# Reordering the opening of a ternary feed-forward kernel: q and W2 in two parts, the weights' sums and transposes placed inside the third and fourth product

## What is computed

```
q   = relu(cond @ W3 + b3)                       # 128 x 256
c   = relu(((32*x + sum_s x) * q[:, None, :]) @ W2 + b2)
wKq = ternary(wK), K = 1, 2, 3: s = mean|w|; clip(round(w / s), -1, 1) * s
out = x + (silu(c @ w1q.T) * (c @ w3q.T)) @ w2q.T
```

## Time and profile before

| | us |
|---|---|
| median of 3 runs | 165.79 (165.62 to 165.82) |
| the profiled execution's own time | 165.22 |
| its span, first to last instruction | 163.4 |
| PE busy | 159.5 (98% of the span) |
| DVE busy | 118.7 (73%) |
| ACT busy | 89.1 (55%) |
| POOL busy | 55.1 (34%) |

### The profile page before, as it was taken

How to read it: one execution, slowest core, us unless ns; L and a number is a source line. 1 busy time by engine, 2 the same in 40 slices (tenths; PEclk the granted TensorE clock), 3 DMA queues, 4 the chain that set the end, 5 groups by cost and what they waited for, 6 DMA issues and landing times.

```text
span 163.4 us, 2290 instructions
## 1 busy us (share of the span) xinstructions
PE 159.5 (98%) x760; PEld 131.0 (80%) x760; DVE 118.7 (73%) x190; ACT 89.1 (55%) x163; POOL 55.1 (34%) x53
## 2 busy tenths in 40 slices
PE   8999999999999999999999999999999999999992
PEld 4798777888887888788887888788887888788892
DVE  1698999988978892798458891788548870566863
ACT  4077889344845375445844475345844466255540
POOL 5014022502460276205750276204841266001500
DMA  5998656665666599200240007000150006000163
GB/s 138 330 337 161 95 83 98 97 98 85 97 98 98 89 201 169 34 4 0 49 79 0 4 0 128 2 0 0 35 96 4 2 0 117 12 0 0 21 112 128
DMA packets 67412, 12.67 MB, mean 78 GB/s; under 512 B 63216, under 2 KB 67144, under 8 KB 67400
## 3 DMA queue, kind: packets, MB, share of 16 engines
q1 hardware_dynamic: 67248, 12.46, 39.2%
q10 hardware_dynamic: 152, 0.07, 0.2%
HBM read 8.32 MB, written 4.19 MB: 77 GB/s over the span
## 4 chain that ended last, share of the span: by engine, by line
PE 97%; DVE 1%; issue 0%; DVEq 0%
PE bank L553 50%; PE bank L596 22%; PE bank L483 15%; PE bank L580 3%; PE bank L469 2%; PE bank L518 1%; PE bank L445 1%; PE bank L498 1%; PE bank L452 1%; PE bank L510 0%; DVE qT L769 0%; PE bank L492 0%; PE bank L443 0%; DVE x L682 0%; DVE xo L821 0%; PE bank L521 0%
## 5 line engine op out<-in xcount | busy, mean ns | idle before, releaser
L553 PE MATMUL bank<-c_hi,T 128*128 128x512 f32 (+1 forms) x176 | 69.2, 393 | 0.0
L553 PE MATMUL bank<-c_lo,T 128*128 128x512 f32 (+1 forms) x176 | 68.8, 391 | 0.0
L389 ACT ACTIVATE silu<-bank,checked 128x512 f32<-128x512 f32 (+1 forms) x48 | 33.1, 689 | 51.5 <-PE bank L553 51.4
L806 DVE SCALAR_TENSOR_TENSOR gf<-bank,out_scale,silu 128x512 f32<-128x512 f32 (+1 forms) x42 | 31.2, 744 | 34.4 <-PE bank L553 30.8
L553 PEld LDWEIGHTS bank<-c_hi,T 128*128 128x128 f32 (+1 forms) x176 | 32.8, 186 | 7.6 <-issue 0.2
L553 PEld LDWEIGHTS bank<-c_lo,T 128*128 128x128 f32 (+1 forms) x176 | 32.8, 186 | 7.3
L272 POOL TENSOR_TENSOR x<-y,qT 128x512 f32<-128x512 f32 x12 | 13.7, 1144 | 53.2 <-DVE y L711 53.2
L596 PE MATMUL bank<-g_hi,T 128*128 128x512 f32 x70 | 28.5, 407 | 0.0
L814 DVE TENSOR_TENSOR g_lo<-gf,g_hi 128x512 fp32r<-128x512 f32 x40 | 28.5, 711 | 0.0
L396 ACT CAST g_hi<-gf 128x512 fp32r<-128x512 f32 x40 | 24.5, 612 | 5.4 <-DVE gf L806 5.1
L596 PE MATMUL bank<-g_lo,T 128*128 128x512 f32 x70 | 27.3, 390 | 0.0
(11 more groups left out here) (81 smaller groups left out, 118.1 us busy)
## 6 DMA issues: line engine op xcount, KB each, us to landing
xb<-in_x_dram SPq DMA_DIRECT2D x64, 64.0 KB, 2.5
out_dram<-turned SPq DMA_DIRECT2D x28, 128.0 KB, 2.7
xo<-in_x_dram SPq DMA_DIRECT2D x3, 256.0 KB, 4.4
w_sb<-in_L_ffn_w_dram SPq DMA_DIRECT2D x2, 384.0 KB, 5.5
w_sb<-in_L_ffn_w_dram SPq DMA_DIRECT2D x1, 682.0 KB, 7.8
w_sb<-in_L_ffn_w_dram SPq DMA_DIRECT2D x2, 256.0 KB
xo<-in_x_dram SPq DMA_DIRECT2D x1, 512.0 KB, 4.7
xo<-in_x_dram SPq DMA_DIRECT2D x2, 128.0 KB, 2.4
```

The costliest lines, as they stand in the source:

```text
L389: nc.scalar.activation(silu[r, m % 2, :], h1[j % 2][r], ACT.Silu, scale=checked[r, 0:1]).then_inc(silu_done, 1)
L553: last = pe.matmul(dst[j % 2][0:w, :], T13[:, k, col:col + w], part[:, g % NC, k, :], start=(i == 0), stop=(i == len(passes) - 1))
L806: nc.vector.scalar_tensor_tensor(out=gf[r, m % 3, :], in0=second, scalar=out_scale[r], in1=silu[r, m % 2, :], op0=ALU.mult, op1=ALU.mult). ...
```

## The change

- SP issues W2 as two loads with a semaphore each, and x half 3 between w1's first and second piece.
- `project_q` takes the sequences it works on. The first call, at its old place, makes q of halves 0 and 1 (16 sequences); the second, of the other 112, takes the place of `keep_busy(3)`. DVE adds bias and relu for the 16, ACT for the 112. `scale_mixed` waits for the latter.
- PE does `sum_partitions(0)` between the two chunks of `project_c(2)`, and w1's first transposes with `sum_partitions(1)` between the two chunks of `project_c(3)`.
- w3's first transposes move behind `h1_step(0)`, then `h1_step(1)`, then `h3_step(0)`, w1's other blocks, `h3_step(1)`, w3's other blocks and `sum_partitions(2)`.
- On DVE `scale_mixed(3)` moves ahead of `limit(0)` and `above_limit(0)`.

```diff
-            def load_w13(w_sb, w, got):
+            def load_w13(w_sb, w, got, between=None):
                 cut = LOADED * P
                 sp.dma_start(w_sb[:, 0:LOADED, :], ...).then_inc(got[0], 16)
+                if between is not None:
+                    load_half(between)
...
-            sp.dma_start(W2_sb[:], ...).then_inc(got_W2, 16)
+            for k in range(DC):
+                sp.dma_start(W2_sb[:, k], W2[k * P:(k + 1) * P, :]).then_inc(got_W2[k], 16)
             load_half(2)
-            load_w13(w1_sb, w1, got_w1)
-            load_half(3)
+            load_w13(w1_sb, w1, got_w1, between=3)
...   (ScalarE, ahead of relu(0))
+            act.wait_ge(q_done, 2 * DC)
+            for c in range(DC):
+                nc.scalar.activation(qT[:, HALVES:NH, c, :], q_rest_ps[:, c]..., ACT.Relu,
+                                     bias=b3_col[c]).then_inc(q_rest_ready, 1)
...   (TensorE, project_c)
                 for c in range(DC):
+                    if c and n == 2:
+                        pe.wait_ge(const_ready, 4)
+                        pe.wait_ge(q_rest_ready, DC)
+                        sum_partitions(0)
+                    if c and n == 3:
+                        pe.wait_ge(x1_done, EARLY - 1)
+                        transpose_w13(0, 0, w1_t)
+                        pe.wait_ge(q_ready, DC)
+                        sum_partitions(1)
...
             mix_x(0)
-            keep_busy(3)
+            project_q(q_rest_ps, slice(QF, B))
             mix_x(1)
-            pe.wait_ge(got_W2, 16)
             project_by_parts(0)
             mix_x(2)
             project_by_parts(1)
             mix_x(3)
-            sum_partitions(0)
             project_c(2)
-            transpose_w13(0, 0, w1_t)
-            sum_partitions(1)
             project_c(3)
-            transpose_w13(1, 0, w3_t)
...
             h1_step(0)
+            transpose_w13(1, 0, w3_t)
+            h1_step(1)
             h3_step(0)
             transpose_w13(0, 1, w1_t)
-            h1_step(1)
+            h3_step(1)
             transpose_w13(1, 1, w3_t)
             sum_partitions(2)
-            h3_step(1)
...   (VectorE)
             early_lo(0)
+            scale_mixed(3)
             limit(0)
             above_limit(0, w1_sb, w1_t, parts[0])
-            scale_mixed(3)
             limit(1)
```

More of the change, by code:

```diff
@@ L53, in adaln_ternary_ffn_kernel @@
     QB = P // BT
+    QF = HALVES * HB
     HTB = HT // BT
@@ L132, in adaln_ternary_ffn_kernel @@
         b_cols_ps = bank[:, 3, 0:2 * DC]
-        qT_ps = bank[:, 5, 0:DC * B].rearrange("p (c b) -> p c b", c=DC)
+        q_first_ps = bank[:, 5, 0:DC * QF].rearrange("p (c b) -> p c b", c=DC)
+        q_rest_ps = bank[:, 4, 0:DC * (B - QF)].rearrange("p (c b) -> p c b", c=DC)
         sums_ps = [bank[:, b, 0:2] for b in (4, 5, 7)]
@@ L146, in z_of @@
             return bank[:, b, :].rearrange("p (c n) -> p c n", c=DC)
-        got_cond, got_W3, got_W2, got_b = sem("got_cond"), sem("got_W3"), sem("got_W2"), sem("got_b")
+        got_cond, got_W3, got_b = sem("got_cond"), sem("got_W3"), sem("got_b")
+        got_W2 = [sem(f"got_W2_{k}") for k in range(DC)]
         got_w1, got_w3 = [[sem(f"got_w{k}_{part}") for part in range(2)] for k in (1, 3)]
@@ L163, in adaln_ternary_ffn_kernel @@
         b_cols_done, b_cols_copied = sem("b_cols_done"), sem("b_cols_copied")
-        q_done, q_ready = sem("q_done"), sem("q_ready")
+        q_done, q_ready, q_rest_ready = sem("q_done"), sem("q_ready"), sem("q_rest_ready")
         abs_done, sums_done, limit_done = sem("abs_done"), sem("sums_done"), sem("limit_done")
@@ L223, in _ @@
             load_half(1)
-            sp.dma_start(W2_sb[:], W2.rearrange("(c p) n -> p c n", p=P)).then_inc(got_W2, 16)
+            for k in range(DC):
+                sp.dma_start(W2_sb[:, k], W2[k * P:(k + 1) * P, :]).then_inc(got_W2[k], 16)
             load_half(2)
             sp.wait_ge(zeroed, 2)
-            load_w13(w1_sb, w1, got_w1)
-            load_half(3)
+            load_w13(w1_sb, w1, got_w1, between=3)
             load_w13(w3_sb, w3, got_w3)
@@ L322, in _ @@
             act.wait_ge(b_cols_copied, 1)
+            act.wait_ge(q_done, 2 * DC)
+            for c in range(DC):
+                nc.scalar.activation(qT[:, HALVES:NH, c, :], q_rest_ps[:, c].rearrange("p (h b) -> p h b", b=HB), ACT.Relu,
+                                     bias=b3_col[c]).then_inc(q_rest_ready, 1)
             def relu(n):
@@ L435, in mix_x @@
                         transpose_b()
-                        project_q()
+                        project_q(q_first_ps, slice(0, QF))
                     if n == 0:
@@ L446, in mix_x, with project_q @@
                 last.then_inc(mixed_done, 1)
-            def project_q():
+            def project_q(q_ps, sequences):
                 pe.wait_ge(got_W3, 16)
@@ L451, in project_q @@
                 for c in range(DC):
-                    pe.matmul(qT_ps[:, c, :], W3_sb[:, c * P:(c + 1) * P], condT[:], start=True, stop=True
+                    pe.matmul(q_ps[:, c], W3_sb[:, c * P:(c + 1) * P], condT[:, sequences], start=True, stop=True
                               ).then_inc(q_done, 1)
@@ L462, in project_by_parts @@
                 for k in range(DC):
+                    if n == 0:
+                        pe.wait_ge(got_W2[k], 16)
                     if k:
@@ L535, in _ @@
             mix_x(3)
-            pe.wait_ge(const_ready, 4)
-            sum_partitions(0)
             project_c(2)
-            pe.wait_ge(x1_done, EARLY - 1)
-            transpose_w13(0, 0, w1_t)
-            pe.wait_ge(q_ready, DC)
-            sum_partitions(1)
             project_c(3)
-            transpose_w13(1, 0, w3_t)
             def hidden_product(m, dst, col, done):
@@ L663, in scale_mixed @@
             def scale_mixed(n):
+                dve.wait_ge(q_rest_ready, DC)
                 if n in SUMMED:
@@ L768, in _ @@
             for c in range(DC):
-                nc.vector.tensor_scalar(qT[:, :, c, :], qT_ps[:, c, :].rearrange("p (h b) -> p h b", b=HB), b3_col[c], 0.0,
-                                        ALU.add, ALU.max).then_inc(q_ready, 1)
+                nc.vector.tensor_scalar(qT[:, 0:HALVES, c, :], q_first_ps[:, c].rearrange("p (h b) -> p h b", b=HB), b3_col[c],
+                                        0.0, ALU.add, ALU.max).then_inc(q_ready, 1)
             dve.wait_ge(q_ready, DC)
```

## The result

| | runs | median us | lowest to highest |
|---|---|---|---|
| before | 22 | 165.68 | 164.86 to 166.14 |
| changed | 22 | 167.41 | 165.15 to 167.97 |
| changed, second time on another occasion | 12 | 166.48 | 164.81 to 167.96 |
| before, beside it | 29 | 165.62 | 164.98 to 167.19 |

A forecast was written before the change was run, and what follows sets the result against it. PE, busy 98% of the span, was taken as the bound, with DVE in step during the opening. Terms 0.33 - 0.18 - 0.11 + 0.04 - 0.18 - 0.08 made it 0.18 us slower: 165.97, say 165.95, range 165.45 to 166.40.

The forecast's parts named there:

- q in two parts, start of the first product: Opening on PE and DVE: q for 16 sequences first lets the first product start at 6.60 to 6.68; gain 0.33 us.
- the term of 0.1: q's records on PE: streaming 16 columns saves 0.1 us, between 0 and 0.33.
- q's split doesn't do what it says: Rival, opening: weight loads hide all savings, the rest of q adds 0.27 to PE; 166.05 us, chance 0.05.
- DVE's q: Opening on DVE: two q instructions of 16 columns take 0.41 us in place of 0.65.
- The 0.07: First product on PE: starting from a running PE, it takes 1.73 us against 1.80.
- Second product: Opening on PE: `x1` of half 1 releases PE at about 8.96, ending at 10.76; 0.18 us of the gain lost.
- w1's threshold: DVE, near 14 us: collides with POOL's low part of half 1, ends 14.52, PE transposes at 14.58; 0.11 us lost.
- w1's second piece: Load issued behind x half 3: lands about 10.2, ACT may wait a tenth; cost 0 until it slips over 1.2 us.
- w3's threshold: DVE, behind `limit(1)`: now alone, takes 0.70 us instead of 1.33, so DVE is late by 0.20 only.
- the wait for w3's signs: PE before `h3_step(2)`: last signs on ACT come late; 0.18 us lost, between 0.05 and 0.3.
- the gain stays: Rival: ACT's signs and DVE's chain are quicker, losses behind 14 us vanish; 165.4 to 165.6 us, chance 0.22.
- DVE falls behind: Rival, at `limit(1)`, 0.83 later: POOL lies across w3's threshold, nothing is repaid; 166.3 to 166.6 us, chance 0.25.

The follow-up runs named there:

- e3: The changed kernel, but PE streams all 128 columns in the first q, of which DVE still takes 16; median 165.59 us, ratio to before 0.9996.
- e14: e9 with the first q streaming 16 columns instead of 128; median 166.88 us.
- e1: The changed kernel with q made whole again at its first place, three fillers behind it; median 165.67 us, ratio to before 0.9993.
- e10: The changed kernel itself run again; six runs from 164.81 to 165.56 us, six from 167.39 to 167.96.
- e8: The kernel before with only q split, its first part streamed whole, old loads and order; median 165.63 us, ratio 0.9996.
- e7: The kernel before with four instead of five 512-column fillers at the start; median 166.31 us, ratio 1.0029.
- e9: e3 with w3's second transposes and w2's sum earlier, and POOL's low part of half 1 waiting for w1's first threshold; median 165.29 us, ratio 0.9970.

## Why the prediction was wrong

**The step that failed** is "q in two parts, start of the first product". It priced every row behind q as in the trace of before, that is at the full pace whatever q does, and asked of the 16 columns only how much time they save. It took the granted clock of 1.00 as given, though q's rows took 0.77 us where later ones took 0.45, and had no rival for a pace that stays low. What the runs showed in its place: q's streaming, just where it stands, decides whether the pace doubles in time. With 128 columns and all five fillers it had by 6.9 us in all seven profiles. With 16 it comes late in 21 of 34 runs of this kernel; then everything from 5.5 to 9.7 us runs at half pace and the execution takes 2.2 us more (e3 and e14, with one size changed in either direction).

**With the pace up in time the rest can be checked step by step on e3.** Its pace doubles at 4.6 us, that of the kernel before at 5.1, so moments agree in part by luck; distances from the start of q in e1 and e3, both at full pace from there on, are the fair comparison.

- First product: forecast 6.68, measured 6.68, and that is luck. q's four records took 0.54 instead of 0.77 because the pace was up, and q began 0.14 later. From the start of q to the product it is 2.04 in e1, with q whole, 1.86 in e3 and 1.87 in e10, with 16 columns. So the split gains 0.18 instead of 0.26, and of it the 16 columns nothing: the term of 0.1 was 0. That is the mechanism of the rival "q's split doesn't do what it says", which had 0.05. DVE's q took 0.44 to the next start (forecast 0.41, before 0.65); this term was right and carries the gain.
- The 0.07 that a product saves by starting from a running PE didn't show: 1.77 in e10 and 1.88 in e3 to the next start, where 1.73 was forecast.
- Second product: forecast 8.96, measured 8.99, again not by the forecast's way. The wait for DVE ahead of it wasn't there: half 2's transposes start at 8.56 and the product 0.43 later, without a wait.
- w1's threshold: forecast 14.52 with PE at 14.58; measured 13.81 and 14.43. The collision with POOL turned out either way: in the first profile POOL was ahead and the threshold took 1.60, in e3 DVE was and POOL paid 0.2. The 0.11 is in one case 0.37 (16.92 - 14.74 against 14.43 - 12.62, from the start of the stretch before w1's transposes) and in the other nothing.
- w1's second piece: forecast to land at 10.2 to 10.3; ACT got it at 10.9, after 0.51 us of waiting. That made POOL later: its subtraction started at 13.45, where 12.7 was forecast, and DVE was first. In the first profile ACT had no such wait, and POOL was first. The edit wasn't free of effects, and e8 shows what x half 3 costs in its old place when PE is early.
- w3's threshold, now alone, took 0.75 instead of 1.33: about right (forecast 0.70).
- w2's sum at 21.00, measured 20.81; its threshold's end 23.29, measured 23.08; w2's transposes 23.35, measured 23.14. The estimate of 1.66 us for the free threshold was 1.64.
- The end: e3's span is 163.5 against 163.4 and its ratio to before 0.9996, where the forecast had 0.18 us slower. Its lead over the kernel before is 0.19 at half 3's mixing (10.72), 0.34 at `h1_step(2)` (21.00, forecast 0.08) and 0.03 at w2's transposes. So a lead was lost there, as forecast, but the terms were mis-sized: `h1_step(2)` took 0.12 more than the 0.92 of before, the wait for w3's signs (forecast 0.18), and `h3_step(2)` to w2's transposes 0.19 more than 0.91 (forecast 0.08).

The lower group looks like the rival "the gain stays": 165.1 to 165.5, ratio 0.9971 (0.9956 to 0.9986) for the six of e10. But it holds only executions with an early pace, and the runs of before beside it aren't chosen so. e3, which needs no such choice, has 0.9996, and e1, with q whole and its pace up at 4.3, has w2's transposes at 22.93 where e10 with 3.8 has 23.02. That the changed kernel keeps a gain isn't shown. The rival "DVE falls behind" didn't happen: g of step 0 ends at 20.6 in e3.

**What stays open.** Why streaming in q's place counts and the same streaming before or behind it doesn't. Four fillers ahead, behind, or on both sides, and the whole product behind, left 4 to 8 upper runs of 11 or 12. e7 shows that the place of q isn't the only one that counts. Nothing in the traces says what decides between two executions of the same program.

## What to carry to other kernels

In an opening that PE spends at its slow pace, a product's streaming isn't idle weight: before thinning work there, compare the spacing of equal records before and after, since a view may print the full clock where the trace has no entry, and take enough runs to see two groups (one profile and three runs could have shown either). If fewer columns are needed early, keep streaming the full width and let the reader of the result take less, as e3 and e9 do; it cost nothing here (0.99 against 1.00 us), because weight loads set the time. And two instructions that share a port trade places for a tenth of a microsecond: a saving that hangs on which one starts first isn't to be counted.

## What the runs showed that I had not expected

- The pace of TensorE doubled anywhere from 3.8 to 10.0 us into the span, and the views give a granted clock of 1.00 for the opening of all of them. A microsecond more at the low pace costs somewhat under half a microsecond: 9.72 instead of 3.78 made the span 166.0 instead of 163.4. Part of the scatter of the kernel before, 164.7 to 167.2, may be this; its executions weren't traced one by one.
- DVE and POOL give way to each other for whole instructions, both ways: DVE's threshold of 0.75 us took 1.60 behind POOL, ending 0.54 after it, about as in the earlier trace rows, and POOL's subtraction of 1.27 took 1.49 behind DVE. The Trainium skill (SBUF — State Buffer, section "SBUF: two separate sides") calls it an exclusive lock for whichever starts first; the traces agree.
